# A mamba-and-experts layer on one core: where a group's first unit splits z's weights, and where it scales and splits the output weights

## What is computed

```python
zxbcdt = hidden_states @ in_proj_w.T
z, xBC, dt = (three slices of it)
xBC = silu(conv_b + sum_i conv_w[:, i] * xBC shifted by i)      # 4 taps
# 64 heads of 64 channels in 8 groups; B and C are shared by a group's 8 heads
M = (C B^T) * exp(dA_cs[i] - dA_cs[j]) * dt[j]                   # lower triangle
y = M x + D * x
y = norm_w * (y * rsqrt(mean(y * y) + eps)) * silu(z)
out = y @ out_proj_w.T
```

## Time and profile before

| what | value |
|---|---|
| runs of the kernel | 1510.77, 7724.07 and 7722.83 us |
| their median | 7722.83 us |
| the profiled execution's span | 1511.5 us |
| granted PE clock, mean | 0.981 |
| PE busy | 1416.6 us, 94% |
| DVE busy | 1192.8 us, 79% |
| ACT busy | 989.4 us, 65% |
| POOL busy | 868.5 us, 57% |

### The profile page before, as it was taken

How to read it: one execution, slowest core, us unless ns; L and a number is a source line. 1 busy time by engine, 2 the same in 40 slices (tenths; PEclk the granted TensorE clock), 3 DMA queues, 4 the chain that set the end, 5 groups by cost and what they waited for, 6 DMA issues and landing times. The chain is left out here.

```text
span 1511.5 us, 25812 instructions
## 1 busy us (share of the span) xinstructions
PE 1416.6 (94%) x7484; PEld 1013.6 (67%) x7484; DVE 1192.8 (79%) x1749; ACT 989.4 (65%) x1450; POOL 868.5 (57%) x758
## 2 busy tenths in 40 slices
PE   4699999999999999999999999999987999999995
PEld 3466667767676776767667677766765667777774
DVE  6799888988997988999898899989757555555556
ACT  4587877878787787877778787877746322333333
POOL 3256676767676666767676676777562143333333
PEclk9799999999999999999999999999988999999998
DMA  4100000010000000000000000000011000000001
GB/s 115 43 13 25 19 18 25 5 33 3 24 18 18 24 3 27 9 24 18 18 25 3 18 18 24 17 18 4 4 57 60 11 11 22 21 21 21 21 0 56
DMA packets 26219, 34.47 MB, mean 23 GB/s; under 512 B 10420, under 2 KB 20276, under 8 KB 26090
## 3 DMA queue, kind: packets, MB, share of 16 engines
q1 hardware_dynamic: 26116, 33.42, 7.3%
HBM read 30.13 MB, written 3.28 MB: 22 GB/s over the span
## 5 line engine op out<-in xcount | busy, mean ns | idle before, releaser
L346 DVE SCALAR_TENSOR_TENSOR acc<-PS,par_a,acc 128x510 f32<-128x510 f32 (+2 forms) x576 | 422.1, 738 | 25.6 <-ACT acc L310 20.0
L1126 POOL TENSOR_TENSOR g_lo<-gy,g_hi 128x512 fp32r<-128x512 f32 x128 | 171.4, 1339 | 215.8 <-ACT g_hi L862 215.7
L1135 POOL TENSOR_TENSOR ssq<-ssq,y 128x256 f32<-128x256 f32 x256 | 262.6, 1026 | 13.2
L1120 POOL TENSOR_TENSOR gy<-y,sz 128x512 f32<-128x512 f32 x128 | 193.4, 1511 | 89.8 <-DVE y L998 57.8
L1736 POOL TENSOR_TENSOR h_lo<-hc,h_hi 128x512 fp32r<-128x512 f32 x68 | 87.6, 1290 | 205.0 <-ACT h_hi L1491 204.9
L985 DVE SCALAR_TENSOR_TENSOR shared<-shared,cbm 128x1024 f32<-128x1024 f32 x96 | 141.4, 1473 | 67.7 <-ACT shared L849 67.6
L310 ACT ACTIVATE acc<-PS,par_a 128x512 f32<-128x512 f32 x192 | 149.3, 777 | 31.2 <-PE PS L293 27.7
L985 DVE SCALAR_TENSOR_TENSOR M<-M,cbm 128x1024 f32<-128x1024 f32 x96 | 150.7, 1569 | 4.9 <-ACT M L849 1.4
L293 PE MATMUL PS<-xnT_hi,wx_hi 128*128 128x512 f32 x384 | 143.3, 454 | 6.5 <-DVE acc L346 5.8
L849 ACT ACTIVATE M<-PS 128x1024 f32<-128x1024 f32 x96 | 98.5, 1026 | 66.8 <-PE PS L687 66.5
L1491 ACT ACTIVATE h_hi<-hc 128x512 fp32r<-128x512 f32 x68 | 43.0, 632 | 151.1 <-DVE hc L1590 151.1
(11 more groups left out here) (198 smaller groups left out, 3194.6 us busy)
## 6 DMA issues: line engine op xcount, KB each, us to landing
wf_raw<-in_wf SPq DMA_DIRECT2D x17, 384.0 KB, 3.1
wraw<-in_wx SPq DMA_DIRECT2D x8, 768.0 KB, 4.5
wraw<-in_wz SPq DMA_DIRECT2D x8, 512.0 KB, 3.4
R<-cs_parts SPq DMA_DIRECT2D x256, 3.0 KB
wraw<-in_wo SPq DMA_DIRECT2D x8, 512.0 KB, 3.4
L<-cs_parts SPq DMA_DIRECT2D x64, 36.0 KB
outT<-in_x SPq DMA_DIRECT2D x4, 512.0 KB, 6.0
shared<-in_x SPq DMA_DIRECT2D x4, 512.0 KB, 3.9
```

What stands on the lines that cost most here:

```text
L346: dve.scalar_tensor_tensor(dst[:, :, s:SEQ], src[:, :, 0:SEQ - s], par_a[:, TAPS * k + TAPS - 1 - s:TAPS * k + TAPS - s], dst[:, :, s:SEQ] ...
L1120: pool.tensor_tensor(gy[:, half, :, :], y[:, half, :, :], sz[:, 2 * half:2 * half + 2, SEQ * b:SEQ * b + SEQ], ALU.mult).then_inc(gy_done, 1)
L1126: pool.tensor_tensor(g_lo[:, cts, ts], gy[:, half, :, :], g_hi[:, cts, ts].bitcast(fp32), ALU.subtract).then_inc(lo_done, 1)
L1135: pool.tensor_tensor(tok, tok, y2[:, half, cc, :], ALU.add).then_inc(ssq_link, 1)
```

## The change

Three things, all in the mamba block:

- ACT, a group's first unit (not in group 0): the four `split_z_hi`, which stood two ahead of the first exponential and two ahead of the second, now stand one at a time: behind the first exponential, behind `tap3` of tile 1, ahead of `z_silu(u, 1)`, and ahead of `tap3` of tile 3. In a group's second unit `split_o` of tiles 2 and 3 moves from ahead of the third exponential to behind it.
- POOL, a group's first unit: the four `split_z_lo`, which were its first work, become one at the start, one behind the first `gate`, and two where `scale_o` stood.
- POOL, a group's first unit (group 0 too): `scale_o` moves from ahead of `gate(u, 0, bt, 0)` to behind `gate`, `gated_lo` and `add_squares(q, 0, bt, 0)`; `split_o` of tiles 0 and 1 follows it directly.

No instruction is added or taken away, and SP's and PE's code stays as it is.

```diff
--- before.py
+++ after.py
@@ -898,39 +898,41 @@
                         if not ahead:
                             last_unit(u)
                             continue
-                        if q == 0 and not first:
-                            for ct in (0, 1):
-                                split_z_hi(act, g, ct)
                         if first:
                             tap3(act, gv, v, 0)
                         decay_exp(0, bt, 0)
+                        if q == 0 and not first:
+                            split_z_hi(act, g, 0)
                         if not first:
                             tap3(act, gv, v, 0)
-                        if q == 0 and not first:
-                            for ct in (2, 3):
-                                split_z_hi(act, g, ct)
                         decay_exp(0, bt, 1)
                         if not first:
                             gated_hi(u - 1, 0, bt - 2, 1)
                         tap3(act, gv, v, 1)
+                        if q == 0 and not first:
+                            split_z_hi(act, g, 1)
                         if not first:
                             square(bt - 2, 1)
+                        decay_exp(0, bt, 2)
                         if q == 1:
                             for ct in (2, 3):
                                 split_o(g, ct)
-                        decay_exp(0, bt, 2)
                         z_silu(u, 0)
                         tap3(act, gv, v, 2)
                         conv_silu(act, vp, v, 0)
                         if not first:
                             gated_hi(u - 1, 1, bt - 1, 0)
                         conv_silu(act, vp, v, 1)
+                        if q == 0 and not first:
+                            split_z_hi(act, g, 2)
                         z_silu(u, 1)
                         bt = 2 * u + 1
                         decay_exp(1, bt, 0)
                         if not first:
                             gated_hi(u - 1, 1, bt - 2, 1)
                             square(bt - 2, 0)
+                        if q == 0 and not first:
+                            split_z_hi(act, g, 3)
                         tap3(act, gv, v, 3)
                         decay_exp(1, bt, 1)
                         tap3(act, gv, v, 4)
@@ -1154,13 +1156,15 @@
                         u = PAIRS * g + q
                         first = isinstance(u, int) and u == 0
                         bt, pq = 2 * u, (q - 1) % PAIRS
-                        if q == 0 and not first:
-                            for ct in range(CT):
-                                split_z_lo(pool, g, ct)
+                        ahead_z = q == 0 and not first
+                        if ahead_z:
+                            split_z_lo(pool, g, 0)
                         if not first:
                             gated_lo(0, bt - 2, 1)
                         if not first:
                             gate(u - 1, 1, bt - 1, 0)
+                            if ahead_z:
+                                split_z_lo(pool, g, 1)
                             add_squares(pq, 0, bt - 2, 1)
                             gate(u - 1, 1, bt - 1, 1)
                             gated_lo(1, bt - 1, 0)
@@ -1173,13 +1177,15 @@
                         if q == 2 and not last:
                             for k in range(3):
                                 split_x_lo(pool, g + 1, k)
+                        if ahead_z:
+                            split_z_lo(pool, g, 2)
+                            split_z_lo(pool, g, 3)
+                        gate(u, 0, bt, 0)
+                        gated_lo(0, bt, 0)
+                        add_squares(q, 0, bt, 0)
                         if q == 0:
                             scale_o(g)
-                        gate(u, 0, bt, 0)
-                        gated_lo(0, bt, 0)
-                        if q == 0:
                             split_o(g, (0, 1))
-                        add_squares(q, 0, bt, 0)
                         if q == 2 and not last:
                             for k in range(3, CONVT):
                                 split_x_lo(pool, g + 1, k)
```

## The result

The changed kernel takes 1517.06 us (median of four runs, 1516.22 to 1520.67). Against the kernel before the ratio is 1.0053, 95% interval 1.0037 to 1.0069: it is slower, by about 8 us, and within 2%. The forecast was 1524, that is 13 us slower. (The 7723 us of two early runs of the kernel before did not come back: in all later runs beside the experiments it took between 1507.8 and 1513.7 us, and all ratios here are against undisturbed runs.)

The account below looks back on a forecast made before the run. The prediction took PE to bound the kernel. 5.5 us won and 18.6 lost gave +13.1 on the span of 1511.5, that is 1524.6, so a time of about 1524 us; range 1508 to 1537.

Parts of the forecast that it names:

- the main case: ACT's wait for POOL's scaling costs 1.3 to 3 us a group; chance 0.56, its own range 1519 to 1531 us.
- Part 3: POOL's scaling behind its additions: ACT waits, the next unit's first exponential is 1.98 us late; 18.6 us lost in all.
- Part 2: SP fetches wo later, with L and R behind it: PE stalls about 0.3 us for R, hidden by the scaling's wait.
- both slower together: Where DVE and POOL work at once both slow down; DVE's chain therefore wins 0.5 us, between 0.20 and 0.74.
- the 0.5 us that the prediction added in groups 2, 3 and 7: Extra loss there because gated_lo starts later behind the unit's middle, making 2.5 us a group in place of 1.98.
- Won: First halves of groups' first units: 0.5 us in five loop groups, 0.9 in groups 1 and 7, 2.06 by clock; 5.5 together.
- Lost in a group: PE's delay at z of tile 1 in a second unit: 1.98 us in four groups, 2.5 in three; 15.4 together.
- Unit 1: Group 0 has no splits of z but has the moved scaling; its table load is 3.2 us later.
- PE and DVE are equally loaded: In a unit's first half, DVE's chain of 8.48 us from the first exponential meets PE again at z of tile 1.
- The rule that the prediction set aside: First starter holds the shared ports, so DVE loses nothing: 0.74 us won per group (group 7: 0.69), sum 1.7 us less, 1522.
- Faster, the first half decides: Rival: ACT finds tile 0 scaled when it comes, only the first halves' win counts; 1505 us, chance 0.08.
- Slower by less: the additions run alone: Rival: POOL's additions do not meet decay_cb; loss 1.0 for 1.98 us in seven groups, 1517 us, chance 0.2.

Follow-up runs that it names:

- the queue turned round: The changed kernel with SP fetching the next unit's L and R ahead of the output weights; ratio 1.0057 to the kernel before.
- both repairs: The changed kernel with scale_o directly behind POOL's gate, additions last, and SP fetching the next unit's L and R ahead of the output weights; ratio 0.9988.
- the last run: The changed kernel with z's last two lo splits ahead of POOL's four additions and the scaling back ahead of the gate; 1505.38 us, ratio 0.9967.
- the scaling alone: The kernel before with only POOL's scaling and first two lo splits of the output weights moved behind the additions; 1529.81 us, ratio 1.0132.

## Why the prediction was right, and where it was wrong

**The sign and the places were right, point by point.** The stop of the loop stayed (2.07 us), PE's first wait fell by 0.72 (0.74 forecast), the clock no longer fell in units 8 and 12, ACT waited at `wo_hi` (4.57 us, 3 to 4 forecast), the silus of z no longer waited for PE, and a new wait stood at the first decay of the second units. That wait was 0.74 us in unit 17 and at most 1.74 elsewhere, where 1.5 to 2 was forecast; with R's 0.46 just ahead of it it is 1.20.

**The size was wrong.** On the profiled span, on which the sum was made, +13.1 us were forecast and +2.9 measured. On the time it looks better, 1517 for 1524, but that is in part luck: the sum took the profiled execution for one like the run of 1510.77, and it was one of about 1513.3. Span 1524.6 would have been a time of 1526.4. The measured 1517 lies inside the wide range, but below the 1519 to 1531 that the main case gave for itself.

**Part 3's schedule was right to 0.15 us.** In unit 16, from the middle of the unit: both splits start 19.52 behind it (629.2 - 609.79 = 19.41 forecast), the table load 21.94 (22.08). The exponential was 1.83 us late (1.98).

**Part 2 was right.** R was waited for, 0.46 us (0.3 forecast), and this is hidden: with the queue turned round the time is the same. It is hidden only behind part 3: with the scaling behind the gate the second halves of groups 2 to 6 were 3.4 us longer by it.

**The step that failed is how DVE and POOL meet, and it stands in both halves of the sum.** The prediction took "both slower together" from two rows, expected the first `decay_cb` to lose by the new split beside it, and held the second ones at their old length. Measured, the first `decay_cb` lost nothing (1.23) while the split beside it took 1.48 us for 0.74, and the second became 0.31 us shorter in unit 16 and 0.41 in unit 17, because they now start nearer to the end of the `gated_lo` that they meet (in unit 16 0.51 us of it was left in place of 0.82). A second term that failed is the 0.5 us that the prediction added in groups 2, 3 and 7 for their later `gated_lo`. So:

- Won: 0.74 + 0.31 = 1.05 for 0.5 us in a loop group; in all 8.5 for 5.5 us (in units 8 and 12 with the clock, 2.16 and 2.00).
- Lost in a group: the exponential's 1.83 less 0.41 is 1.42 us, which is what groups 2 to 6 show (1.40 to 1.43 over the two halves), for 1.98 or 2.5. In groups 1 and 7 it is 2.16 and 1.79. In all seven 11.0 for 15.4 us. Of the 4.4 us between them 2.9 (0.41 in each of seven) are the shorter second `decay_cb`. The other 1.5 are the exponential, late by 13.9 us in sum and not 15.4: 2.59 in group 1, 1.81 to 1.84 in groups 2 to 6, 2.21 in group 7. The added 0.5 us did not come in groups 2 and 3, where `gated_lo` was late only in halves behind a fall of the clock: with the clock up, their second halves run as that of group 4 (19.94 and 19.93 us against 19.91).
- Unit 1: 2.8 for 3.2 us.

Together +5.3 in the block for +13.1. The runs differ by 8 us and the profiled spans by 2.9. The 2.4 us between the spans and the block lie outside the units that the change touches; most of the 5 us between the spans and the runs is that the profiled execution of the kernel before was one of its slower ones. If most of its executions had no fall of the clock, the 2 us won back by the clock are no part of what the runs show.

One reading of the prediction does not follow from its rows: that PE and DVE are equally loaded in a first half. In unit 17's PE is busy for 13.13 us and DVE for 10.60; what holds there is only that DVE's chain from the first exponential to tile 1 has no gap.

**The rule that the prediction set aside was the right one.** It quoted the Trainium skill ("SBUF — State Buffer", section "SBUF: two separate sides", on port arbitration: the one that starts first has the shared ports for its whole instruction) and held the row at 626.82 against it, a `decay_cb` of 1.77 us. That row is the rule at work: POOL's second `wo_lo` was under way when it started and ended at 627.50, and 627.50 + 1.08 = 628.58 is its end. The two rows were two meetings with different firsts, not one meeting with both losing. With the rule the sum would have been 1.7 us lower as quoted, and with the rule applied to the shifted second `decay_cb` too, about 4.4 us lower still (an estimate: 0.31 us in the first units of groups 2 to 6 and 0.41 in all seven second units). That is 6.1 of the 7.8 us by which the sum was off in the block; the rest is mostly the 1.5 us of the exponential.

**The rivals.** "Faster, the first half decides" did not happen, but its cause was real and worth 8.5 us. "Slower by less: the additions run alone" gave 1517, which is the time measured, by a cause that did not occur: the additions took 2.56 us in unit 16. The clock fell in none of the seven groups after the change; the new waits there are at most 1.74 us. In unit 1 PE stood 2.75 us in three runs, and the clock fell in two of them, not in the changed kernel's profile.

## What to carry to other kernels

Moving work out of a bound stretch pays what it says there; look then at what each moved piece was a condition for. Here z's splits were what let the shared buffer be refilled, so moving them moved a transfer, a scaling, another engine's wait and a queue, and only putting the last two splits as early as their inputs allow made the first gain stand. Before placing an instruction of one of two engines that share a port, compute from the trace which of them will be under way when the other starts, and how much of it will be left; here a shift of 0.6 us in the start of POOL's gate cost DVE 0.6 us, and where both started within 0.02 us of each other the order fell differently from group to group. So look at these meetings in every group and not in one, and keep them apart by more than that.

## What the runs showed of the hardware

- A `decay_cb` (a DVE instruction with two SBUF operands) that starts while POOL has an instruction under way takes the rest of POOL's plus 1.08 us. Of the 192 in the run with both repairs 77 started with POOL idle or within 0.1 us of the end of its instruction and took 1.22 us in the median, none over 1.23, though POOL's next instruction began during 52 of them; the other 115 took rest + 1.08 or 1.09 us. POOL's pays in the other order: its gate takes 2.27 us in place of 1.28 (604.78 in the changed kernel). Where the trace has POOL start 0.01 to 0.03 us ahead of DVE it does not tell who waits: in groups 2 and 6 of the last run, and once in the kernel before (893.03), DVE went first all the same. The sum of the waits is 57 us in the kernel before, and 51 in the changed one (all `decay_cb`, less 1.222 us each).
- The granted PE clock, 0.90 in the mean over the half in which it fell (0.50 in part of that half, as in unit 8), did so behind idle times of PE of 2.3 to 2.8 us, and not always (2.29 in unit 16 before: no; 2.27 there with the scaling alone: yes). Behind 1.85 us or less it fell in none of the runs' first and second units of groups 1 to 7. One fall costs about 1.0 us (17.00 against 16.02 for the first halves of units 16 and 20 with the scaling alone, behind 2.27 us of idle time in both).
- ACT stands 2.0 to 2.4 us at the turn of the loop over groups, in every kernel here, and none of these edits touches it. It makes up the 1.9 us that first halves in the loop still take over 13.13: in groups 1 and 7, where this stop is absent, the changed kernel's take 13.21 and 13.15.
